# Layer 1 attention, first group: the exponential moved between value moves, the value bias row moved among the next group's fills

## The reference, cut to what matters

```python
qkv = jnp.einsum('sbf,pf->sbp', src, in_proj_weight) + in_proj_bias
q, k, v = jnp.split(qkv, 3, axis=-1)
q = to_heads(q) / np.sqrt(d)
attn = jax.nn.softmax(jnp.einsum('nsd,ntd->nst', q, k), axis=-1)
out = jnp.einsum('nst,ntd->nsd', attn, v)
out = out @ out_proj_weight.T + out_proj_bias
...
x = _layernorm(x + _L1_attn_ref(x, ...), axis=-1)
```

## Time and profile before

| what | value |
|---|---|
| median of 3 runs | 2253.92 us (2253.87 to 2260.16) |
| the profiled execution, its own time | 2256.29 us |
| its span | 2254.2 us |
| layer 1 attention in the span | about 529 to 889 us |
| mean granted TensorE clock, whole span | 0.951 of full speed |

### The profile page before, as it was taken

How to read it: one execution, slowest core, us unless ns; L and a number is a source line. 1 busy time by engine, 2 the same in 40 slices (tenths; PEclk the granted TensorE clock), 3 DMA queues, 4 the chain that set the end, 5 groups by cost and what they waited for, 6 DMA issues and landing times. The chain is left out here.

```text
span 2254.2 us, 35996 instructions
## 1 busy us (share of the span) xinstructions
PE 1992.2 (88%) x12788; PEld 1422.9 (63%) x12788; DVE 1534.8 (68%) x2463; ACT 1151.3 (51%) x2215; POOL 960.5 (43%) x740
## 2 busy tenths in 40 slices
PE   7898877997988885899999999999999997699997
PEld 4565546995653554556666656565666664599996
DVE  5677854555788896688788768887787886322223
ACT  3332311111358456678775867677776773233333
POOL 2233232222232141266666656675666665222223
PEclk9999988998899997999999999999999998799998
DMA  4100007312000001000100000000000001631113
GB/s 158 39 23 23 23 26 294 136 36 108 0 1 0 1 30 65 3 1 1 30 1 1 10 30 1 1 10 1 1 1 1 10 1 45 237 110 36 39 36 124
DMA packets 37158, 95.63 MB, mean 42 GB/s; under 512 B 5492, under 2 KB 24696, under 8 KB 32248
## 3 DMA queue, kind: packets, MB, share of 16 engines
q1 hardware_dynamic: 31032, 77.07, 9.4%
q0 software_dynamic: 5952, 16.26, 2.2%
HBM read 78.89 MB, written 14.42 MB: 41 GB/s over the span
## 5 line engine op out<-in xcount | busy, mean ns | idle before, releaser
L2217 POOL TENSOR_TENSOR x_total<-x_total,x_pt 128x1024 f32<-128x1024 f32 x189 | 446.4, 2362 | 173.9 <-ACT x_pt L2303 155.9
L2325 ACT ACTIVATE x_pt<-PS,x_maskf 128x512 f32<-128x512 f32 x544 | 332.1, 689 | 165.7 <-PE PS L2639 164.7
L2424 DVE TENSOR_TENSOR PS<-x_pt,PS 128x512 f32<-128x512 f32 x480 | 333.3, 694 | 65.3 <-ACT x_pt L2325 28.4
L2442 DVE TENSOR_TENSOR x_pt<-x_pt,PS 128x1024 f32<-128x1024 f32 x320 | 320.2, 1051 | 0.7 <-PE PS L2657 0.7
L2639 PE MATMUL PS<-x_qs,x_ks 64*128 64x256 f32 x2176 | 280.3, 394 | 1.5 <-ACT x_pt L2325 1.5
L2616 PE MATMUL PS<-x_pt,x_vs 128*64 128x256 f32 x2108 | 262.4, 388 | 20.4 <-ACT x_pt L2303 10.6
L2303 ACT ACTIVATE x_pt<-x_pt 128x1536 f32<-128x1536 f32 (+1 forms) x160 | 266.5, 1667 | 13.3 <-DVE x_pt L2442 13.3
L1163 PEld LDWEIGHTS PS<-m_xT,m_own 128*128 128x128 f32 x1984 | 234.7, 195 | 8.2 <-DVE m_own L1243 2.9
L1163 PE MATMUL PS<-m_xT,m_own 128*128 128x128 f32 x1984 | 235.7, 278 | 4.1 <-DVE m_own L1243 2.4
L2639 PEld LDWEIGHTS PS<-x_qs,x_ks 64*128 64x128 f32 x2176 | 198.5, 188 | 64.0 <-issue 38.6
L2616 PEld LDWEIGHTS PS<-x_pt,x_vs 128*64 128x64 f32 x2108 | 142.0, 137 | 137.4 <-issue 64.0
(11 more groups left out here) (321 smaller groups left out, 2921.0 us busy)
## 6 DMA issues: line engine op xcount, KB each, us to landing
f_w<-in_L_ffn_w SPq DMA_DIRECT2D x32, 1024.0 KB, 6.1
a_ctxT<-in_ctxT SPq DMA_DIRECT2D x8, 800.5 KB, 4.4
l_w<-in_ctx SPq DMA_DIRECT2D x4, 1024.0 KB
f_w<-ys SPq DMA_DIRECT2D x16, 256.0 KB, 5.5
l_w<-in_L_attn_w SPq DMA_DIRECT2D x6, 512.0 KB, 6.2
a_xT<-in_xT SPq DMA_DIRECT2D x4, 512.0 KB, 5.9
X<-in_x SPq DMA_DIRECT2D x1, 2048.0 KB, 11.3
xr<-a_xn SPq DMA_DIRECT2D x16, 128.0 KB, 1.7
```

The source lines that it names most:

```text
L2217: ins = nc.gpsimd.tensor_tensor(total2[:], first, tile[:, 2 * k + 2:2 * k + 4, :], ALU.add)
L2325: nc.scalar.activation(pt[:, s % 2, t, :].rearrange("p (h n) -> p h n", h=2), PS[:, first:first + 2, half], ACT.Identity, bias=maskf[:, b ...
L2424: ins = nc.vector.tensor_tensor(acc, tile, acc, ALU.max)
L2442: nc.vector.tensor_tensor(p_, p_, PS[:, MB, None, :].to_broadcast([P, at.stop - at.start, SPAN]), ALU.subtract).then_inc(lowered, 1)
```

## The change

It does four things, all in the first or last group:

- ScalarE: `exponent(0)` stands behind the third value move of group 0, ahead of the other five.
- TensorE: the value bias row is a function of its own, `value_row`, and stands among the fills of group 1, behind use 10; `fold_biases` keeps only the folded weights.
- VectorE: the addition that makes `vb` and raises `vb_ready` stands behind the scores of group 1, where it stood behind those of group 0.
- GpSimd: `residual_input` runs one group later; that of the last group stands behind `rstd(pool, J - 2)`, ahead of the statistics of the context.

What is not touched is the wait of the first `project` of group 0 for `vb_ready`.

```diff
@@ gpsimd
                 bias_terms(grp)
-                residual_input(grp)
+                if grp >= 1:
+                    residual_input(grp - 1)
             rstd(pool, J - 2)
+            residual_input(J - 1)
             pool.wait_ge(c_stats, 1)
@@ scalar
                 move(0, u)
...
-            exponent(0)
+                if u == VF + 2:
+                    exponent(0)
             for grp in range(J - 1):
@@ vector
                 now = sc[:, grp % 2]
-                if grp == 0:
+                if grp == 1:
                     dve.wait_ge(small_loaded, 48)
                     dve.wait_ge(vb_done, 1)
                     nc.vector.tensor_tensor(vb[:], PS[:, PB + 1, 0:D], bo[:], ALU.add).then_inc(vb_ready, 1)
@@ tensor
                 mm.then_inc(fold_done, 1)
+
+            def value_row():
+
                 pe.wait_ge(wo_loaded, 16)
...
                     for u in range(VF):
                         fill(grp + 1, u)
+                        if grp == 0 and u == TURNED + 2 * B:
+                            value_row()
```

More of the change, by code:

```diff
@@ L1628, in turned @@
                                PS[:, OB:OB + 2, :].rearrange("p b n -> p (b n)")).then_inc(oT_ready, 1)
[L1630 to L1634, removed]
             def weigh_to(grp, made, end):
@@ L1642, in exponent @@
                 nc.scalar.activation(sc[:, grp % 2], sc[:, grp % 2], ACT.Exp, scale=HD1 ** -0.5).then_inc(ex_ready, 1)
-            exponent(0)
+            for u in range(USES):
+                if u == QK:
+                    act.wait_ge(fold_done, 1)
+                    nc.scalar.copy(fold[:], PS[:, PB, 0:KD * AB + H1]).then_inc(fold_ready, 1)
+                move(0, u)
+                if u == VF + 2:
+                    exponent(0)
             for grp in range(J - 1):
```

## The result

| | kernel before | changed kernel |
|---|---|---|
| median | 2254.57 us (2253.87 to 2260.16, 4 runs) | 2273.21 us (2270.59 to 2276.14, 4 runs) |
| profiled execution, its own time | 2256.29 us | 2272.10 us |
| its span | 2254.2 us | 2270.0 us |

The ratio is 1.0072, with a 95% interval of 1.0057 to 1.0087, so the kernel is some 16 us slower (13 to 20). The spans differ by 15.8 us, the medians by 18.6.

The account below looks back on a forecast made before the run. TensorE's projections and value fills were taken as the bound, VectorE's scores close behind. 13.0 (wait) + 1.2 (restart) + 2.1 (end) = 16.3 us on the median 2253.92 gave 2270.2 us, range 2262 to 2276.

Parts of the forecast that it names:

- Use 18: TensorE, group 0: without the row ahead, it waits only for the folded weights' copy and starts 6.0 us earlier.
- the later of the two returns: TensorE, group 0: full clock returns at 591.5, not 587.6, so the value fills lose 3.0 us and end 1.3 earlier.
- rival 1: Group 0: the clock returns early, the projection starts 11.0 to 8.3 us later, total 2262 to 2268 us; chance 0.24.
- S: How far ahead ScalarE gets in group 0: 6.9 us (5.3 + 1.3 + 0.3); 8.9 and 11.6 with other clock ends.
- The row in its new place: TensorE, fills of group 1: the row costs nothing, covered by a lead of some 7 us; uncovered 3.3 to 6.6.
- The wait: First projection of group 0 stands 20 us for `vb_ready` behind group 1's scores, starting 13.0 us later than before.
- The restart: After standing, TensorE restarts the first projection of group 0 at the low clock: +1.2 us, ends 0 and 3.0.
- The addition in group 1: GpSimd's group 0 addition beside VectorE's score bias of group 1 costs that some 1.7 us, covered by later value fills.
- The end of the stage: GpSimd's last addition runs beside VectorE's two normalizations and stretches them: +2.1 us, ends 0 and 2.4.
- the lasting low clock: TensorE stays slow through all value fills of group 0, sum about 27 us, 2281 us, or through the projections; chance 0.06.
- the blocked ring: Group 0: the early exponential stalls the value fills, its gain falls towards 0, sum 23 us, 2277 us; chance 0.03.
- the wait is no wait: VectorE makes `vb` before TensorE reaches the first projection: not slower, -4.8 us, 2249.1 us; chance 0.03.

Follow-up runs that it names:

- `exp_late`: Changed kernel with only the exponential of group 0 put back behind all eight value moves; ratio 1.0106 to the kernel before, stage 335.0 us.
- `wait_third`: Changed kernel with TensorE's wait for `vb` at the third projection of group 0 instead of the first; ratio 1.0037 to the kernel before, stage 323.3 us.
- `tail_early`: Changed kernel with the last group's GpSimd addition ahead of the last but one group's deviations; ratio 1.0056 to the kernel before, stage 327.7 us.
- `exp_only`: Kernel before with only the exponential of group 0 moved behind the third value move; ratio 0.9956 to the kernel before, stage 308.9 us.
- `row_dealt`: `exp_only` with the row's matmuls dealt among the folding's narrow ones in singles and pairs; ratio 0.9994 to the kernel before, stage 312.2 us.
- `tail_only`: Kernel before with only the last group's GpSimd addition moved behind the last but one group's deviations; ratio 1.0021 to the kernel before, stage 314.9 us.
- `vb_mid`: Changed kernel with VectorE's addition making `vb` moved ahead of the fifth pair of group 1; ratio 0.9970 to the kernel before, stage 308.3 us.
- `row_first`: `exp_only` with the whole value bias row ahead of the folded weights; ratio 1.0000 to the kernel before, stage 309.7 us.

## Why the prediction was right

The forecast of 2270.2 us lay 3.0 under the measured median and inside 2262 to 2276; for the profiled execution it gave 2272.6, and that took 2272.1 us. That the two meet within 0.5 us is partly luck: the stage grew by 17.0 us where 16.3 were forecast, and the span by only 15.8. The folding started 0.9 us earlier in the trace after than in that before (568.21 against 569.10), so I take that off below.

- **Use 18** starts at 581.41, 6.7 us earlier, 5.8 without the offset; 6.0 were forecast.
- **The clock in group 0.** The later of the two returns was right. The clock had fallen while the narrow matmuls ran, at 573.9 before and 572.9 after, 4.7 to 4.8 us behind the first of them. The granted clock is 0.51 in the microsecond from 589 and full from 590, 5.2 us behind the first value fill (6.0 forecast). Stretches of TensorE in the changed kernel, the last two for the restart below:

```profile
588.00:589.00 1.00, 1.00 (x2) 0.50 0.00 0
589.00:590.00 1.00, 1.00 (x2) 0.51 0.00 0
590.00:591.00 1.00, 1.00 (x4) 1.00 0.00 0
...
671.00:672.00 1.00, 1.00 (x4) 0.55 0.00 0
672.00:673.00 1.00, 1.00 (x8) 1.00 0.00 0
```

  The value fills end 2.4 us earlier, 1.5 without the offset; 1.3 forecast. Of the 5.8 us that the row's removal freed, the low clock took 4.3. The choice was right for this trace and not for every one: with the same matmuls up to there the clock came back 5.0 to 5.9 us behind the first value fill in `exp_late`, `wait_third` and the three kernels that make `vb` amid the scores, but after 2.6 us in `tail_early`:

```profile
585.00:586.00 1.00, 1.00 (x3) 0.80 0.00 0
```

  This early return, of the kind of rival 1, shortens the value fills from 16.54 to 15.27 us.
- **ScalarE's idle time** is gone whole, and TensorE reaches its second turn at 644.64 instead of 652.74: 7.2 us earlier without the offset, S = 6.9 forecast.
- **The row in its new place** takes 3.62 us at the full clock, and TensorE makes the five fills behind it without a pause, so it used its lead and cost nothing.
- **The wait** is 19.68 us, released by `l_vb` (20 forecast). The projection starts 11.8 us later, 12.7 without the offset, for 13.0.
- **The restart** is the one term that was mis-sized. I took +1.2 from the last group's projection, and it was 6.47 - 4.29 = +2.2; the full clock came 5.6 us behind the start (the microsecond from 671 shows 0.55, that from 672 the full clock). In two experiments with the same idle time ahead the projection took 5.77 and 5.47, which makes 1.2 to 2.2 over three traces. The row that the 1.2 came from is no fixed number either: the first projection of the last group took 4.35 to 5.73 us over all traces. And not all of it is the price of the long wait, for the same projection took 5.38 in `exp_only` and 5.55 in `row_dealt`, where TensorE did not wait for `vb`.
- **The addition in group 1** had cover, as forecast, but it hit another instruction than forecast: the score bias took 0.41 us, and the subtraction of the maximum behind it 1.82 instead of 0.42.
- **The end of the stage** cost 2.0 for 2.1, and the order of starts was the unfavourable one. `tail_only` shows the price alone.
- **Groups 2 and 3** carried the delay on unchanged: 14.0 at the value fills of group 1, 14.0 at the normalizations.

The sum without the offset is 12.7 + 2.2 + 2.0 = 16.9, the stage's 17.0. Of the rivals, the early return of the clock (for this execution), the lasting low clock and the blocked ring all fell by the trace of the changed kernel; that the wait is no wait fell with the 19.68 us. Its price was sound in kind, as `vb_mid` shows: where VectorE makes `vb` in time, the kernel is faster than before by 5.1 us in the stage, for -4.8 worked out.

## What to carry to other kernels

When a piece of work is moved to a later place, look up who waits for its result, and where that waiter stands: here the row's matmuls moved into free time, but their consumer on VectorE was put behind 30 us of other work while TensorE's wait for it stayed. A wait that was free is not moved by a diff, and so it does not show in it. In this kernel a GpSimd addition was cheap or dear by what VectorE did beside it: put it beside the statistics or the reductions, not beside the elementwise work.

## What the runs showed of the hardware

- GpSimd's addition of 2.35 us stretched two `TENSOR_SCALAR` of VectorE from 0.74 to 2.75 us and a `TENSOR_TENSOR` from 0.42 to 1.83, and left thirteen `BATCH_NORM_STATS2` at 4.33 us. Beside it in group 1 of the changed kernel, a `TENSOR_REDUCE` took 0.59 us, 0.58 without it.
- TensorE was busy without a pause when the granted clock fell from 1.00 to 0.50, 2.9 to 5.2 us into the narrow matmuls. It stayed full through 11 us of mixed narrow and wide matmuls (two of 256 columns behind eight of 16) and fell 5.0 us into a mixture with half as many wide ones, in one trace each. I had expected the finer mixture to do better.
- TensorE time freed behind the narrow matmuls was worth much less than its length: 4.3 of 5.8 us went to the low clock in the changed kernel, 3.0 of 6.2 in `tail_early`, and in `row_first` 2.5 freed turned into 1.9 lost.
